# A two-sequence transformer block: the weight test's maximum on TensorE, transfers reordered, first FFN tokens made one chunk earlier

## The reference, cut to what matters

```python
x = x + attention(layernorm(x), Wq, bq, Wk, bk, Wv, bv, Wo, bo)   # rotary positions, causal softmax
h = layernorm(x)
g = (h @ gate_w.T) * gate_s
u = (h @ up_w.T) * up_s
x = x + ((silu(g) * u) @ down_w.T) * down_s
```

## Time and profile before

| | |
|---|---|
| median of three runs | 833.29 us |
| profiled execution, own time | 835.75 us |
| its span | 833.7 us |
| TensorE busy | 766.5 us (92%) |
| VectorE, ScalarE, GpSimd busy | 449.6, 307.9, 246.6 us |
| C1 on TensorE | 512.65 to 579.40 us of the span |
| FFN | from 581.04 us to the end |

### The profile page before, as it was taken

How to read it: one execution, slowest core, us unless ns; L and a number is a source line. 1 busy time by engine, 2 the same in 40 slices (tenths; PEclk the granted TensorE clock), 3 DMA queues, 4 the chain that set the end, 5 groups by cost and what they waited for, 6 DMA issues and landing times.

```text
span 833.7 us, 10625 instructions
## 1 busy us (share of the span) xinstructions
PE 766.5 (92%) x3520; PEld 532.9 (64%) x3520; DVE 449.6 (54%) x1102; ACT 307.9 (37%) x637; POOL 246.6 (30%) x224
## 2 busy tenths in 40 slices
PE   4889999989999999999999999936999999999996
PEld 3677787755554545454555545825888888888885
DVE  5848393787666767776777734736214214314112
ACT  3221213155554555554555563201323222222221
POOL 0323252511114141414141416641223223223223
PEclk9999999998999999999999999978999999999999
DMA  8285576544556555555575535940000100001001
GB/s 276 76 303 186 202 235 241 218 146 133 142 143 167 143 165 146 160 143 143 144 187 149 134 100 172 372 169 1 1 1 13 38 1 31 19 0 48 5 0 53
DMA packets 52012, 104.37 MB, mean 125 GB/s; under 512 B 14820, under 2 KB 15332, under 8 KB 51444
## 3 DMA queue, kind: packets, MB, share of 16 engines
q1 hardware_dynamic: 51960, 103.72, 40.0%
HBM read 69.62 MB, written 38.21 MB: 129 GB/s over the span
## 4 chain that ended last, share of the span: by engine, by line
PE 77%; DVE 8%; issue 8%; DMA 3%; POOL 2%; ACT 2%; SPq 1%; DVEq 0%; POOLq 0%; ACTq 0%
PE ps L1014 31%; PE ps L1131 17%; PE ps L1038 12%; PE ps L1203 9%; PE ps L1112 6%; DVE masked L780 2%; PE ps L1006 1%; DMA x_st<-in_x 1%; POOL xr L538 1%; DMA us_sb<-in_us 1%; DVE row_max L780 1%; ACT xT_hi L572 1%; DVE oT_lo L930 1%; DVE st_lo L846 1%; DVE xn L742 0%
## 5 line engine op out<-in xcount | busy, mean ns | idle before, releaser
L646 ACT ACTIVATE p<-ps 128x384 f32<-128x384 f32 (+3 forms) x384 | 170.4, 492 | 145.5 <-PE ps L1112 143.1
L1038 PE MATMUL ps<-k_st,q_st 96*128 96x512 f32 (+2 forms) x384 | 142.1, 392 | 15.6 <-DVE row_max L780 8.8
L1131 PE MATMUL ps<-p,v_slot 128*64 128x512 f32 (+3 forms) x768 | 148.0, 509 | 1.2 <-ACT o_raw L653 1.2
L780 DVE CUSTOM_DVE_ANT_0 masked<-ps,mask_qk 128x512 bf16<-128x512 f32 (+1 forms) x240 | 112.7, 503 | 51.0 <-PE ps L1038 49.8
L1112 PE MATMUL ps<-q_st,k_st 99*128 99x384 f32 (+2 forms) x384 | 129.8, 359 | 1.4 <-ACT p L646 1.1
L1038 PEld LDWEIGHTS ps<-k_st,q_st 96*128 96x128 f32 x384 | 71.8, 193 | 91.9 <-issue 36.4
L973 DVE SCALAR_TENSOR_TENSOR hid<-ps,us_sb,silu 128x512 f32<-128x512 f32 x44 | 33.0, 751 | 169.0 <-PE ps L1014 166.5
L557 POOL TENSOR_TENSOR hid_lo<-hid,hid_hi 128x512 fp32r<-128x512 f32 x44 | 56.7, 1290 | 180.0 <-ACT hid_hi L717 180.0
L522 POOL TENSOR_SCALAR_AFFINE_SELECT p<-p 128x512 f32<-128x512 f32 x64 | 40.6, 634 | 225.9 <-ACT p L646 225.9
L782 DVE TENSOR_REDUCE row_max<-ps 128x1 f32<-128x512 f32 (+1 forms) x128 | 83.5, 655 | 38.6 <-PE ps L1038 35.7
L1131 PEld LDWEIGHTS ps<-p,v_slot 128*64 128x64 f32 x768 | 46.7, 138 | 66.9 <-issue 58.0
(11 more groups left out here) (93 smaller groups left out, 1080.6 us busy)
## 6 DMA issues: line engine op xcount, KB each, us to landing
qk_scratch<-st_hi SPq DMA_DIRECT2D x32, 512.0 KB, 3.8
q_st<-qk_scratch SPq DMA_DIRECT2D x32, 384.0 KB, 4.5
k_st<-qk_scratch SPq DMA_DIRECT2D x32, 384.0 KB, 5.3
flag_st<-in_ffn SPq DMA_DIRECT2D x32, 264.0 KB, 2.8
ffn_copy<-in_ffn SPq DMA_DIRECT2D x32, 264.0 KB, 3.2
qk_scratch<-st_lo SPq DMA_DIRECT2D x16, 512.0 KB, 4.1
o_T<-o_raw SPq DMA_DIRECT2D x32, 128.0 KB, 2.7
rec_l<-rec_rows SPq DMA_DIRECT2D x32, 128.0 KB, 3.3
```

Of the source, the lines that this page charges most:

```text
L646: act.activation(p32[:, at:at + q0 + w - keep], ps[:, ST_BANK + i % RING, keep - q0:w], ACT.Exp, scale=SCALE).then_inc(exp_done, 1)
L780: ins = dve.tensor_tensor_reduce((masked_a if u < 2 else masked)[:, s_before(i) % 2, col:col + kept], scores, mask_qk[:, 512 - kept:512], ...
L1038: ins = pe.matmul(ps[:, S_BANK + i % RING, col:col + w], q_st[0:K_DOT, slot, qt * P:(qt + 1) * P], k_st[0:K_DOT, slot, k0:k0 + w], start=T ...
L1131: ins = pe.matmul(ps[VW * a:VW * (a + 1), O_BANK + half, q0 - 512 * half:512], v_slot[:, slot, kt, :], p32[:, at:at + n], start=(kt == 0), ...
```

## The change

The maximum over the partitions is no longer GpSimd's: TensorE transposes the 128 values into one row of PSUM bank 5 after chunk 0, and VectorE reduces that row before chunk 1's tiles. Both `xr` loads now stand in front of the up and down weights. `xst_c` moves to the memory of the `wo` staging buffer. The first chunk's tokens are normalised tile by tile among chunk 2's tiles on VectorE, and TensorE transposes each before the product of chunk 3's tile instead of after it; ScalarE and VectorE take up the transposed tile without waiting for that product.

```diff
-        flag_all = sb("flag_all", [P, 1], F32)
+        with ExitStack() as after_wo:
+            xst_c = sb("xst_c", [P, TJ, H], F32, after_wo)
...
-            xst_c = sb("xst_c", [P, TJ, H], F32, after_o)
...
-            for m, (dst, done) in enumerate(((wg_sb, gate_in), (wu_sb, up_in), (wd_sb, down_in))):
+            def load_ffn(m, dst, done):
                 sp.dma_start(dst[...], ffn_copy[...]).then_inc(done, 16)
-                if m < CC:
-                    sp.wait_ge(x2_ready, TJ * (m + 1))
-                    load_x(xr[:, m, :, :], CC + m).then_inc(xr_in[CC + m], 16)
+            load_ffn(0, wg_sb, gate_in)
+            for k in range(CC):
+                sp.wait_ge(x2_ready, TJ * (k + 1))
+                load_x(xr[:, k, :, :], CC + k).then_inc(xr_in[CC + k], 16)
+            load_ffn(1, wu_sb, up_in)
+            load_ffn(2, wd_sb, down_in)
...
             add_bias(1)
-            pool.wait_ge(flag_done, HEADS + 1)
-            pool.partition_all_reduce(flag_all[:, :], flag_part[:, :], P, ReduceOp.max).then_inc(flag_ready, 1)
-            pool.wait_ge(flag_ready, 1)
-            pool.tensor_copy(flag_int[:, :], flag_all[:, :]).then_inc(flag_ready, 1)
             add_bias(2)
...
                 for j in range(TJ):
-                    act.wait_ge(o_ps, TJ * c + j + 1)
                     if c + 1 < N_CH:
+                        act.wait_ge(o_ps, TJ * c + j + 1)
                         o_hi(c + 1, j)
                     else:
                         transposed_hi(N_CH, j)
...
             for c in range(N_CH):
+                if c == 1:
+                    dve.wait_ge(flag_T, 1)
+                    dve.tensor_reduce(flag_int[0:1, 0:1], ps[0:1, FLAG_BANK, 0:P], AX_X, ALU.max).then_inc(flag_ready, 1)
+                if c == N_CH - 2:
+                    dve.wait_ge(wo_lo_done, 1)
+                    dve.wait_ge(ln_rstd, N_CH + 1)
                 for j in range(TJ):
+                    if c + 1 == N_CH:
+                        transposed_lo(N_CH, j)
                     ... x2 = product + xr
                     if c + 1 < N_CH:
                         o_lo(c + 1, j)
-                    else:
-                        transposed_lo(N_CH, j)
+                    if c == N_CH - 2:
+                        token_tile(0, j)
                     ... statistics
-                if c == N_CH - 2:
-                    tokens(0)
...
+                    if c + 1 == N_CH:
+                        if j == 0:
+                            pe.wait_ge(o_evac, 2 * PAIRS)
+                            pe.wait_ge(flag_ready, 1)
+                        pe.wait_ge(x2_tokens, j + 1)
+                        transpose_tile(N_CH, j, xst_c[:, j, :])
                     ... product(ps[:, j, :])
-                    if c + 1 == N_CH:
-                        ... the same transposes, without the wait for flag_ready
+                if c == 0:
+                    pe.wait_ge(flag_done, HEADS + 1)
+                    pe.transpose(ps[0:1, FLAG_BANK, 0:P], flag_part[:, :], ident[:, :]).then_inc(flag_T, 1)
...
-            pe.wait_ge(flag_ready, 2)
+            pe.wait_ge(flag_ready, 1)
             inexact = pe.value_load(flag_int[0:1, 0:1])
```

More of the change, by code:

```diff
@@ L208, in transformer_block @@
             x2_1 = sb("x2_1", [P, KT, H], F32, after_o)
-            xst_c = sb("xst_c", [P, TJ, H], F32, after_o)
         o_T = sb("o_T", [P, GROUPS, S], F32)
         ps = ctx.enter_context(nc.psum_tensor("ps", [P, 8, 512], F32))
-        T_BANK, MM_BANK = 0, 4
+        T_BANK, MM_BANK, FLAG_BANK = 0, 4, 5
         S_BANK, ST_BANK, O_BANK = 0, 3, 6
@@ L287, in transformer_block @@
         x2_ready = sem("x2_ready")
+        flag_T = sem("flag_T")
         flag_ready = sem("flag_ready")
@@ L543, in _ @@
             add_bias(1)
-            pool.wait_ge(flag_done, HEADS + 1)
-            pool.partition_all_reduce(flag_all[:, :], flag_part[:, :], P, bass.bass_isa.ReduceOp.max).then_inc(flag_ready, 1)
-            pool.wait_ge(flag_ready, 1)
-            pool.tensor_copy(flag_int[:, :], flag_all[:, :]).then_inc(flag_ready, 1)
             add_bias(2)
@@ L934, in _, with token_tile @@
             reciprocals(GROUPS - 1)
+            def token_tile(c, j):
+                if c > 0:
+                    dve.wait_ge(t_ps, TJ * (N_CH + c - 1) + j + 1)
+                normalize(N_CH + c, j, xst_c[:, j, :], x2_tile(c, j)).then_inc(x2_tokens, 1)
             def tokens(c):
                 for j in range(TJ):
-                    if c > 0:
-                        dve.wait_ge(t_ps, TJ * (N_CH + c - 1) + j + 1)
-                    normalize(N_CH + c, j, xst_c[:, j, :], x2_tile(c, j)).then_inc(x2_tokens, 1)
+                    token_tile(c, j)
             for c in range(N_CH):
+                if c == 1:
[4 more added lines that the diff above has]
+                    dve.wait_ge(ln_rstd, N_CH + 1)
                 for j in range(TJ):
+                    if c + 1 == N_CH:
+                        transposed_lo(N_CH, j)
                     dve.wait_ge(o_ps, TJ * c + j + 1)
```

## The result

The changed kernel took 807.56 us (median of four runs, 804.74 to 815.4) against 833.28 before. The ratio is 0.9708, with a 95% interval of 0.9636 to 0.978. More runs of both came with the experiments. Over all of them, profiled executions left out, the kernel before takes 832.2 us (the 46 runs beside the experiments, standard error 0.5) and the changed one 809.6 us (16 runs, 0.6). That is 22.6 us off, less than the 25.7 between the two medians above, and still more than the 18.7 of my sum.

The account below looks back on a forecast made before the run. TensorE, busy 92%, could gain only where it stood, around GpSimd's all-reduce; VectorE became the new bound. Moving the FFN's start from 581.04 to 562.3 took 18.7 us off 833.29, giving 814.6 us, range 810.5 to 819.5.

Parts of the forecast that it names:

- the all-reduce's part: On GpSimd: 17.2 us of standing lie around the all-reduce; without it add_bias(2) can start 17.8 us earlier.
- The date of the FFN: When the FFN's first matmul starts: forecast at about 562.3 instead of 581.04 us, with nothing edited after it.
- +1.2 for two: VectorE, chunk 1: two rest parts now meet GpSimd's add_bias, so the chunk ends at 542.2, not 541.0.
- my 12.65: VectorE, chunk 2: 9.65 us of own work plus 3.0 of contention with GpSimd, ending at 554.9.
- my 3.8: TensorE: its gaps of 12.32 and 5.16 us close, and one of about 3.8 us comes before the FFN.
- Rival (a): TensorE sets the FFN's start because VectorE keeps up: FFN at 559.5, 21.5 us off, 811.8; chance 17%.
- +0.6 to +0.8: VectorE, chunk 2: extra us for each of four or five contended instructions beside GpSimd, +3.0 in all.
- clock full throughout: Sign of being right: TensorE's clock does not fall, listed beside no TensorE gap between 512 and 558.
- rival (b): VectorE's contention is dearer (821.0), or TensorE's clock falls in the new gap, costing 1.4 us (816.0); chance 13%.
- a gain in one is taken as the same gain in the other: The profiled execution's gain, 18.7 us, is taken over unchanged to the median.
- the later weights would cost nothing: Loads: up weights land at 551.1 and down at 557.8, both with over 10 us to spare.
- what `xr` 3 gains: Loads: the reordering is worth what it takes from chunk 3's residual rows, landing at 544.4 instead of 545.5.

Follow-up runs that it names:

- flag_only: The kernel before with only the maximum moved from GpSimd to TensorE and VectorE, loads and tokens as before; 814.78 us, ratio 0.9802.
- all_but_flag: The changed kernel with the all-reduce put back on GpSimd between add_bias(1) and add_bias(2); 827.36 us, ratio 0.9947.
- old_loads: The changed kernel with loads in the old order, up weights ahead of chunk 3's residual rows; run twice, 813.81 and 809.81 us.
- fill8: The changed kernel with 8 matmuls nobody reads in TensorE's gap ahead of the FFN; run twice, 810.56 and 808.42 us.
- tail: The changed kernel with chunk 2's square root behind three transposed tiles and two of chunk 3's statistics behind the last sum; 808.04 us, ratio 0.9702.
- old_loads_tail: The changed kernel with the old order of the loads, and the square root and two statistics moved as in tail; 808.74 us, ratio 0.9705.
- tail_fill4: The kernel of tail with 4 idle matmuls in what is left of the gap ahead of the FFN; 809.67 us, ratio 0.9734.
- before_third: The kernel before, unedited, run a third time; 827.96 us.

## Why the prediction was right and wrong

*What bounds the kernel, and the all-reduce's part.* Right. The stalls go when the reduce and its copy go (flag_only) and come back with them (all_but_flag). They were 17.2 to 18.8 us in four profiles of before.

*The date of the FFN.* Right, in mechanism and in size. I forecast 562.3 on a span in which C1 began at 512.65, so 49.65 us from C1 to FFN. The four profiles show 48.58 to 50.07. (In the first the FFN begins at 558.45, ahead of my "560 to 565", because C1 began 2.8 us earlier.) By terms, in the first of them: chunk 1 on VectorE slipped by one contended rest part (1.76 instead of 0.68; I had +1.2 for two). Chunk 2 took 11.9 us for my 12.65: two normalised tiles at 1.52 and 1.51 and a wait of 0.30 for ScalarE, while all four rest parts ran at 0.68 to 0.69, where I had wanted them over 1 us. ScalarE's hand-over 0.84 for my 1.0. Chunk 3 6.1 for 6.2. The gap was 2.7 to 3.9 for my 3.8. Rival (a), TensorE as the bound, did not happen: it waited for VectorE each time.

By the Trainium skill's rule ("SBUF — State Buffer", "Who interferes with whom"), the normalisation's two-port mode contends with GpSimd, and whichever issues first holds the shared ports for its whole instruction while the other blocks. The trace agrees. The normalised tile of 544.99 began inside GpSimd's tile of 544.45 to 546.22 and ended 0.29 us after it. The rest part of 544.39 began 0.06 us ahead of that GpSimd tile and took its lone 0.68; there the GpSimd tile paid, 1.77 us instead of 1.30. So a meeting costs VectorE what is left of GpSimd's tile, or nothing where VectorE is first. My flat +0.6 to +0.8 for each was an average over such cases, and that it came out near (2.0 in chunk 2 for 3.0) is in part luck: which tiles meet shifts from profile to profile.

*The clock.* Missed: I had named "clock full throughout" as a sign of being right. I gave the fall to rival (b), at a gap of 3.8 us, as unlikely and at 1.4 us. It happened in all four profiles, at gaps of 2.7 to 3.9, and cost 0.8 to 2.8 us (FFN to end 253.3 to 255.25 against 252.5). I had leaned on the first gap of before, and misread it: a mean clock of 0.66 over 550 to 552 puts the fall at 550.6, 5.1 us after TensorE stopped, not 5.7. And I had left out the second gap, where TensorE stopped at 562.3 and the clock fell 2.0 us later:

```profile
564.00:566.00 2.00, 0.00 (x0) 0.00 (x0) 2.00 (x3) 0.00 (x0) 2.00 (x2) 0.57 0.00 0
```

I had also sized it from a restart of one product, 12 matmuls; here 14 matmuls at 0.43 instead of 0.23 are 2.8. With the mean fall of 1.9, the forecast for the profiled executions is 18.7 less 1.9, so 16.8; C1 to end fell by 17.6.

*What failed.* The step from the profile to the time: "a gain in one is taken as the same gain in the other", with a scatter of 1.4 us taken from three runs. The 18.7 held in the profiles (17.6 from C1 on, with the clock's fall in it); the timed gain was 25.7 in the first comparison, where my range stopped at 22.8. Over all runs it is 22.6, at the very edge. Single runs of both kernels scatter with a standard deviation of 2.4 to 3.5 us. In the first comparison the changed kernel's three unprofiled runs were on the low side (806.6 on average; 808.3, 810.4 and 811.4 in the later ones). Against the 809.6 of all of them, that is 3.0 us of the miss of 7.0.

Where the rest lies is not shown. Each version's gain can be read twice: from C1 to end in its profile, against the mean of before, and from its unprofiled runs, against those of before that ran beside them (standard error 0.9 to 2.1):

| kernel | off C1 to end, profile | off the time, unprofiled |
|---|---|---|
| changed (4) | 17.5, 17.2, 18.6, 17.1 | 26.5, 24.7, 21.5, 19.0 |
| flag_only | 18.1 | 17.9 |
| all_but_flag | 1.2 | 4.4 |
| old_loads (2) | 21.5, 21.5 | 20.2, 21.1 |
| fill8 (2) | 21.0, 19.8 | 21.7, 21.0 |
| tail | 21.3 | 24.2 |
| old_loads_tail | 21.0 | 24.6 |
| tail_fill4 | 21.3 | 21.8 |

The changed kernel gains more timed than in its profile all four times, by 1.9 to 9.0 us, 5.3 on average; the four differ so much that the standard error is near 1.8. That the clock's fall is missing in unprofiled executions would explain 1.9 of it, 2.8 at most. For it: of the kernels without the fall, flag_only, old_loads, fill8 and tail_fill4 agree within 1.4 us, and all_but_flag, which has it, gains 3.2 more timed. Against it: tail and old_loads_tail have no fall and still gain 2.9 and 3.6 more timed, and fill8, 3 us shorter than the changed kernel by the profiles, averages 809.8 us (11 runs), the same. The recorded mean clock, 0.986 unprofiled and 0.984 profiled in the changed kernel, is too close to tell. So the mechanism of the forecast was right. The difference between the profiled and the timed gain, some 5 us and known to about 2, stays open.

*The loads.* I said the later weights would cost nothing, and that held: the up weights, issued at 537.8, landed 13.2 us later, at 551.0, with the FFN's start at 558.45. I said the order would bring what `xr` 3 gains. It brought nothing: `add_bias(3)` was needed late, and by the profiles starting it early put it beside VectorE's critical chunk.

## What to carry to other kernels

A cross-partition reduce on GpSimd can cost far more than its own row: here 0.38 us of work stood between 5.5 to 7.7 us and 9.7 to 11.8 us of unnamed standing in five profiles, and whatever is queued behind it pays. Look at idle time on both sides of a rare instruction, above all where an "issue" wait passes through it on the chain. Starting a helper's work as early as possible need not be free: where GpSimd's tiles met VectorE's, once VectorE was the bound, one of the two waited for the other. And before a forecast to a few microseconds, look at how much of the span scatters with no edit at all, and take the scatter from more than three runs.

## What the runs showed of the hardware that I had not expected

- Gaps of TensorE ahead of the FFN of 0.26 to 2.17 us did not bring the clock to its lower level, in eight profiles of edited kernels and four of before; gaps of 2.68 to 3.93 us saw it fall, in all five. Elsewhere in C1 it held through the 3.40 us of flag_only, and through one of 3.57 us in before_third, to fall 0.4 us after TensorE had started again. The 14 falls in C1 came 2.0 to 5.1 us after TensorE had stopped, so a gap of 2.7 to 3.9 us can go either way.
- A rest part beside `scale_group` (1024 columns on GpSimd) took 2.85 us, against 0.68 alone. It began 0.10 us after GpSimd's instruction and ended 0.55 us after it, so it waited for all that was left of it:

```profile
522.75 2.40 POOL L517 TENSOR_TENSOR o_T<-o_T,rec_l 128x1024 f32<-128x1024 f32 x1 [1.66 <-DMA rec_l<-rec_rows]
```

```profile
522.85 2.85 DVE L932 TENSOR_TENSOR oT_lo<-o_T,oT_hi 128x512 fp32r<-128x512 f32 x1
```

- The profile of tail_fill4 has a granted clock of 0.95 where others have 1.00, in nearly every stretch (0.935 on average over the span). Its FFN took 252.95 us, 0.6 more than tail's.
